# Context projections in feature blocks of 128 and 64, two batches' rests side by side in the array, and a reordered way into layer f1

## The chip, the cores and the metric

The kernel runs on one core of a Trainium2 chip. The metric is the device time of one launch in microseconds (us), the median of several runs. The engines are TensorE (PE), VectorE (DVE), ScalarE (ACT), GpSimd (POOL) and SyncE (SP, which issues most transfers); the profile also has PEld, the weight loads of TensorE.

## The reference

Two blocks of a gated cross-attention network over 8 batches of 100 tokens with 256 features, and a context of 361 rows with 192 features per batch. What the change touches, cut to its core:

```python
# block 0: cross-attention on the layer-normed tokens
q = x @ Wq + bq                                  # 16 heads of 16
k = y @ Wk + bk ; v = y @ Wv + bv                # y: (8, 361, 192), Wk and Wv: (192, 256)
attn = softmax(q k / 4) ; out = relu((attn v) @ W1 + b1) @ W2 + b2
# then a top-1 mixture of 8 experts (256 -> 1024 -> 256)
# block 1: bitnet_linear(x, W, b): int8 activations (one scale for the whole tensor), ternary weights
vis = bitnet_linear(y, W_d2v)                    # 192 -> 256
image = bitnet_linear(vis, W_img) ; fused = bitnet_linear(x, W_txt)
for Wa in (W_att0, W_att1): kv = bitnet_linear(image, Wa) ; fused += 0.1 * softmax(fused k) k
h = relu(bitnet_linear(concat(fused, mean(image)), W_f1)) ; bitnet_linear(h, W_f2)
# then attention whose q, k, v, o are mixtures of 16 experts
```

## The kernel before

Every engine has its own instruction stream, written out by hand; semaphores join them. There is no scheduler: the order in the code is the order on each engine.

**The front** (the first 61 us). SP issues the loads in the order keys' weights `w_k`, context of batch 0, values' weights `w_v`, batch 1, tokens `x`, batches 2 and 3, constants, `w_q`, batches 4 to 5 and 6 to 7, then the ternary layers' weights. The context lies transposed in `ctx_a`, its 192 features in two blocks (k = 0, 1) of `KC` = 96 partitions. TensorE makes the keys of a batch in two halves m (`project_keys`, a 128x361 output each) and the values in three chunks `CH` of some 120 context rows (`project_values`, 121x256 each). Each of these five outputs of a batch takes two fp32 matmuls, one for each feature block; the profile shows each fp32 matmul as two instructions. The outputs go round banks 0 to 3, and ACT copies each out (`context_keys_out`, `context_values_out`). Batches 0 to 3 come first, with the transposes of the normalised tokens (`turn_tokens`) in between, then the queries, then batches 4 to 7 with the score waves of batch 0 between them. `score_wave(b, w)` makes four score blocks of 100x361 at the same time, each on 32 of the array's 128 rows and in a bank of its own; DVE takes maxima from them (`score_maxima`), and the next wave waits for these. `split_maxima` makes three bf16 parts of the maxima, `turn_maxima` transposes them. After batch 0's split, DVE also makes the ternary form of `f2`.

Meanwhile DVE makes the layer norm of the tokens, the largest absolute context value (`ctx_maximum`), the ternary weights, and the quantised context `qc` (`quantise`: a pass into fp32, a pass into bf16). POOL spreads the queries of a batch over head blocks (`spread_q`).

**The loop** (61 to some 190 us): for n = 0 to 9, `score_pair` (two 64-row matmuls of 400 columns side by side, fp32, then two in bf16 from `rows_bf`), the four waves of the next batch, `values`, and between them up to six `chain_unit`s: the d2v layer (16 units, each two bf16 matmuls from `qc`, K = 96) in n = 0 to 2 and the img layer in n = 5 to 7.

**Into f1** (381 us). DVE adds the last attention outputs to `fT` (`add_out`), takes their maximum (`token_maximum`), POOL reduces it over the partitions, DVE rounds tokens and the mean of the image (`qavg`) and f1's 16 outputs follow on TensorE, each four bf16 matmuls: two from `qx`, two from `qavg`. `keep_busy(0, 8)` has TensorE do 8 matmuls that nobody reads while it waits.

## Time and profile before

| | us |
|---|---|
| three runs | 598.03, 600.60, 601.18 (median 600.6) |
| the profiled execution's own time | 597.44 |
| its span, first to last instruction | 595.3 |
| TensorE busy in the span | 579.1 (97%) |
| VectorE, ScalarE, GpSimd busy | 385.1 (65%), 219.2 (37%), 138.2 (23%) |

A timeline line gives the start and the length of a merged run of equal instructions, the engine, the source line, the output and inputs by name, the shape, and how many; in square brackets stands how long the engine was idle before it and which instruction ended that. Lengths of matmuls overlap, since they are pipelined, so the time that a piece takes is read from one start to the next.

### The profile page before, as it was taken

Reading aid. Unit: us, or ns where it says so; the run is one execution under the profiler, and the core shown is the slowest. Engines: PE = TensorE matmul, PEld = TensorE weight load, DVE = VectorE, ACT = ScalarE, POOL = GpSimd, SP = SyncE. Lnnn points to the kernel's source line nnn. Section 1 sums busy time; section 2 is a strip of 40 time slices with the busy share of each in tenths; the row PEclk is TensorE's granted clock in tenths of the full one; section 3 lists DMA queues with packets and bytes.
Section 4 is the critical chain, followed back from the end, with each engine's and each line's share of the span. In section 5 each row is a group of like instructions: output and inputs, shape, how many; then the busy total and the mean of one; then the engine's idle time right before and its main releaser. Section 6 shows DMA issues by size and latency. Waiting matters only on the chain.

```text
span 595.3 us, 10362 instructions
## 1 busy us (share of the span) xinstructions
PE 579.1 (97%) x3975; PEld 429.9 (72%) x3975; DVE 385.1 (65%) x928; ACT 219.2 (37%) x513; POOL 138.2 (23%) x172
## 2 busy tenths in 40 slices
PE   9989999999999999999999989999999999999997
PEld 7756344454456767999999748767787888887587
DVE  2895767587884865222222579887999779775454
ACT  3554656566673464222222376585210010001000
POOL 0052201114003402222222000004355565440000
PEclk9999999999999999999999999999999999999999
DMA  8920000012000662999998200610743663320000
GB/s 193 325 87 1 18 2 1 4 35 57 2 1 22 207 216 69 312 339 354 350 340 276 64 1 1 207 42 2 243 139 96 209 220 95 106 80 0 1 28 29
DMA packets 25694, 71.07 MB, mean 119 GB/s; under 512 B 5270, under 2 KB 13062, under 8 KB 21814
## 3 DMA queue, kind: packets, MB, share of 16 engines
q1 hardware_dynamic: 21910, 58.15, 29.7%
q0 software_dynamic: 3744, 12.38, 6.3%
q8 instruction: 27, 0.44, 0.3%
q14 instruction: 13, 0.11, 0.1%
HBM read 65.02 MB, written 5.49 MB: 118 GB/s over the span
## 4 chain that ended last, share of the span: by engine, by line
PE 83%; DVE 12%; ACT 3%; issue 2%; POOL 1%; DVEq 0%; POOLq 0%
PE bank L1666 12%; PE bank L2190 10%; PE bank L1998 8%; PE bank L2011 8%; PE bank L1821 8%; PE bank L2268 7%; PE bank L2178 6%; PE bank L1795 5%; PE bank L1839 3%; PE bank L1764 2%; PE bank L1827 2%; PE bank L1645 1%; DVE nmax L1063 1%; PE bank L2118 1%; PE bank L2115 1%
## 5 line engine op out<-in xcount | busy, mean ns | idle before, releaser
L2190 PEld LDWEIGHTS bank<-region,kvT 128*128 128x128 f32 x448 | 77.0, 190 | 9.9 <-issue 0.9
L2190 PE MATMUL bank<-region,kvT 128*128 128x200 f32 x448 | 81.1, 333 | 0.8 <-DVE region L1180 0.8
L761 DVE TENSOR_REDUCE nmax<-bank 100x2 f32<-100x722 f32 x64 | 55.2, 905 | 24.9 <-PE bank L1795 24.6
L1998 PEld LDWEIGHTS bank<-stage,region 128*128 128x128 f32 x448 | 52.1, 192 | 1.4 <-issue 0.8
L1998 PE MATMUL bank<-stage,region 128*128 128x128 f32 x448 | 52.4, 275 | 0.5 <-ACT stage L1490 0.5
L2011 PE MATMUL bank<-region,stage 128*128 128x256 f32 x224 | 50.7, 379 | 0.0
L2178 PE MATMUL bank<-region,kvT 128*128 128x400 f32 x128 | 48.5, 502 | 0.6 <-DVE region L1187 0.6
L2011 PEld LDWEIGHTS bank<-region,stage 128*128 128x128 f32 x224 | 41.5, 190 | 5.0
L2268 PE MATMUL bank<-region,kvt 128*128 128x200 f32 (+1 forms) x192 | 44.5, 389 | 0.3 <-DVE region L1247 0.3
L977 DVE TENSOR_SCALAR stage<-bank,stage 128x128 f32<-128x128 f32 x56 | 15.8, 344 | 43.6 <-PE bank L1998 43.6
L554 POOL TENSOR_TENSOR kvT<-kvT 128x256 f32<-128x256 f32 x32 | 27.6, 863 | 54.9 <-DMA kvT<-in_p_qkv 47.7
L1513 ACT ACTIVATE stage<-bank,stage 128x128 f32<-128x128 f32 x56 | 16.0, 368 | 66.1 <-PE bank L1998 66.1
L2268 PEld LDWEIGHTS bank<-region,kvt 128*128 128x128 f32 x192 | 33.5, 190 | 9.0 <-DVE region L1247 0.6
L1821 PE MATMUL bank<-xT,kvt 64*121 64x400 f32 (+1 forms) x144 | 37.9, 545 | 0.7 <-ACT region L1469 0.4
L470 POOL PARTITION_ALL_REDUCE scol<-scol x5 | 1.8, 361 | 142.2 <-DVE scol L753 46.8
L1247 DVE TENSOR_TENSOR region<-region,stage 128x200 f32<-128x200 f32 (+1 forms) x48 | 20.3, 435 | 18.8 <-PE bank L2268 18.8
L2178 PEld LDWEIGHTS bank<-region,kvT 128*128 128x128 f32 x128 | 23.1, 190 | 10.9 <-issue 1.1
L1187 DVE TENSOR_TENSOR region<-xT,stage 128x800 f32<-128x800 f32 x30 | 30.8, 1026 | 0.1
L1469 ACT ACTIVATE region<-bank 121x400 f32<-121x400 f32 (+1 forms) x48 | 21.8, 501 | 19.8 <-PE bank L1827 19.8
L983 DVE TENSOR_TENSOR stage<-bank,stage 128x256 f32<-128x256 f32 x14 | 5.9, 425 | 35.6 <-PE bank L2011 35.6
L1469 ACT ACTIVATE kvT<-bank 121x400 f32<-121x400 f32 (+1 forms) x48 | 21.8, 501 | 19.2 <-PE bank L1827 19.2
L526 POOL DMA_INDIRECT y_slots<-stage,token_of x13 | 13.0, 996 | 67.4 <-DVE stage L983 67.4
(360 smaller groups left out, 1097.0 us busy)
## 6 DMA issues: line engine op xcount, KB each, us to landing
region<-in_e_w SPq DMA_DIRECT2D x28, 1024.0 KB, 6.2
kvT<-in_p_qkv SPq DMA_DIRECT2D x32, 384.0 KB, 3.1
stage<-w_dram POOLq DMA_DIRECT2D x2, 1600.0 KB, 13.3
stage<-in_t_f SPq DMA_DIRECT2D x1, 2048.0 KB, 14.6
kvt<-in_p_o SPq DMA_DIRECT2D x1, 2048.0 KB, 9.0
stage<-in_e_b SPq DMA_DIRECT2D x14, 128.0 KB, 6.6
region<-in_ctxT SPq DMA_DIRECT2D x3, 541.5 KB, 13.5
stage<-w_dram POOLq DMA_DIRECT2D x3, 400.0 KB, 4.8
```

The lines of the kernel that those rows point to most:

```text
L554: pool.tensor_tensor(s[:, 0:2, :], w[:, :, HE:2 * HE], w[:, 0, 0:2 * HE].rearrange("p (i n) -> p i n", i=2), ALU.subtract).then_inc(S["poo ...
L761: dve.tensor_reduce(nmax[:, b % 2, at_h:at_h + 9:8], banks[0:N, bank:bank + 2, 0:M], AX.X, ALU.max, negate=True)\
L1187: dve.tensor_tensor(x_w[n % NW], xT[:, :, at_h], w_bc[h][:, None, e, :].to_broadcast([P, 2, HT]), ALU.mult).then_inc(S["xw_done"], 1)
L1469: act.activation(probsT[n % 2][0:rows_c, c, g].rearrange("p j n -> p (j n)"), psum[4 + y % 3][0:rows_c, 0:4 * N], ACT.Exp).then_inc(S["y_o ...
L1666: ins = pe.matmul(bank, w(k), src(k), start=start and k == 0, stop=stop and k == kk - 1)
L1795: ins = pe.matmul(psum[i + (4 if b == 0 else 0)][0:N, 0:M], qm[b % 3][at_i, t, 2 * (i % 2) + par, :], kT[at_i, t, b, :], start=True, stop= ...
L1821: pe.matmul(bank[g], kT[at_g, t, b, c0:c0 + rows_c], qm[b % 3][at_g, t].rearrange("p j n -> p (j n)"), start=True, stop=False)
L1998: ins = pe.matmul(psum[2 * u + m // 4][:, (m % 4) * P:(m % 4 + 1) * P], e_w1[u][:, k, m * P:(m + 1) * P], xsT[u][:, k, :], start=k == 0, s ...
L2011: ins = pe.matmul(psum[4 + u][:, 0:D], hsT[u][:, m, :], e_w2[u][:, m, :], start=m == 0, stop=m == KF - 1)
L2178: ins = pe.matmul(psum[V_BANK[h]][:, 0:HT], p_w[n % NP][:, k, 2 * HE:3 * HE], x_w[n % NW][:, k, :], start=e == 0 and k == 0, stop=e == E1 ...
L2190: return pe.matmul(bank, left, right, start=e == 0 and i % 2 == 0, stop=e == E1 - 1 and i in (1, 3, 5, 6))
L2268: ins = pe.matmul(psum[LAST_BANK[part] + m][:, at_p], o_all[:, e, m * P:(m + 1) * P], z_w[n % NW][:, at_p], start=e == 0, stop=e == E1 - 1)
```

## The change

The 192 features stand in a block of 128 (`ctx_f`, all 8 batches) and a rest of 64 (`ctx_r`). Rests of even batches lie on partitions 0 to 63, those of odd batches on 64 to 127, and the rest of each weight (`w_k`, `w_v`, d2v) is loaded twice, once for each half. `pair_of_banks` works on a pair of batches: two 128-row matmuls into two banks, then the two rests on the two row halves. The order of loads is now: both batches of pair 0, `w_v`, `x`, pair 1, constants, `w_q`, pairs 2 and 3; ACT issues seven of the first loads. The context's maxima and its quantisation go over 128 partitions and 12 blocks of 361 columns instead of 96 partitions and 16 blocks. The d2v units use a 128-row and a 64-row matmul. TensorE no longer waits for `q_out` before pair 2, and `turn_maxima(0)` stands ahead of the first wave of batch 1. The last part changes the way into f1. The diff, cut:

```diff
+KR = DT - P
-for _name, _p, _w in (("d2v", KC, 512), ("img", P, 512), ("txt", P, 512), ("att0", P, 256),
+for _name, _p, _w in (("d2v", P, 512), ("img", P, 512), ("txt", P, 512), ("att0", P, 256),
-CTX_PARTS = ((0, 1), (1, 2), (2, 4), (4, 6), (6, 8))
+PAIRS = B // 2
+CTX_PART = (0, 1, 2, 2)
+        ctx_f = region[:, 0:B * M].rearrange("p (b m) -> p b m", b=B)
+        ctx_r = region[:, B * M:ctx_w].rearrange("p (r m) -> p r m", r=PAIRS)
 # SP
+            def load_context(part, b0, b1):
+                sp.dma_start(ctx_f[0:KC, b0:b1], d["ctxT"][:, 0, b0:b1]).then_inc(S[f"ctx_in{part}"], 16)
+                sp.dma_start(ctx_f[KC:P, b0:b1], d["ctxT"][0:P - KC, 1, b0:b1]).then_inc(S[f"ctx_in{part}"], 16)
+                for s in range(2):
+                    sp.dma_start(ctx_r[s * KR:s * KR + KR, b0 // 2:b1 // 2], d["ctxT"][P - KC:KC, 1, b0 + s:b1:2])\
+                        .then_inc(S[f"ctx_in{part}"], 16)
+            sp.dma_start(w_a[0:KC, 512:768], d["w_a"][0:KC, 512:768]).then_inc(S["ctx_in0"], 16)
+            sp.dma_start(ctx_f[0:KC, 0:2], d["ctxT"][:, 0, 0:2]).then_inc(S["ctx_in0"], 16)
+            for s in range(2):
+                sp.dma_start(ctx_r[s * KR:s * KR + KR, 0], d["ctxT"][P - KC:KC, 1, s]).then_inc(S["rest_in0"], 16)
...
 # DVE
-            layernorm(ins)
-            for part in range(1, len(CTX_PARTS)):
-                ins = ctx_maximum(part)
-            link(ins)
+            layernorm(ins, lambda: ctx_maximum(1))
+            link(ctx_maximum(2))
-            quantise(qc[0:KC], ctx_a[0:KC], kvT[0:KC, :, :, :], 0, KC).then_inc(S["quantised"], 1)
+            quantise(stage[:, 4096:6984].bitcast(BF16)[:, 0:ctx_w], region[:, 0:ctx_w], kvT_cols[:, 0:ctx_w], 0)\
+                .then_inc(S["quantised"], 1)
-                if 4 <= n < 2 * B + 4:
-                    add_out(dve, n - 4)
                 if n >= 5:
                     g = n - 5
                     if g < B:
                         token_sum(g)
                     else:
                         ins = token_maximum(g - B)
+                if 4 <= n < 2 * B + 4:
+                    add_out(dve, n - 4)
...
-            dve.tensor_scalar(half_of(q_tmp, 0), half_of(fT, 0), scol[:, 19:20], MAGIC, ALU.mult, ALU.add)
+            link(dve.tensor_scalar(half_of(q_tmp, 0), half_of(fT, 0), scol[:, 19:20], MAGIC, ALU.mult, ALU.add))
+            dve.tensor_scalar(half_of(qx, 0), half_of(q_tmp, 0), MAGIC, None, ALU.subtract)\
+                .then_inc(S["half_rounded"], 1)
             dve.tensor_scalar(avg[:, :, :], avg[:, :, :], scol[:, 19:20], MAGIC, ALU.mult, ALU.add)
             output_scale(16, ("f1",))
-            dve.tensor_scalar(qavg, avg[:, :, :], MAGIC, None, ALU.subtract)
-            dve.tensor_scalar(half_of(qx, 0), half_of(q_tmp, 0), MAGIC, None, ALU.subtract)\
-                .then_inc(S["half_rounded"], 1)
+            dve.tensor_scalar(qavg, avg[:, :, :], MAGIC, None, ALU.subtract).then_inc(S["half_rounded"], 1)
 # PE
+            def pair_of_banks(r, unit, rows_c, width, left, right):
+                for s in range(2):
+                    j = 10 * r + 2 * unit + s
                     if j >= 4:
                         pe.wait_ge(S["ctx_out"], j - 3)
+                    pe.matmul(psum[j % 4][0:rows_c, 0:width], left(slice(0, P), 0, 2 * r + s),
+                              right(slice(0, P), 0, 2 * r + s), start=True, stop=False)
+                if r == 0 and unit == 0:
+                    pe.wait_ge(S["rest_in0"], 64)
+                for s in range(2):
+                    j, at_s = 10 * r + 2 * unit + s, slice(s * KR, s * KR + KR)
+                    pe.matmul(psum[j % 4][0:rows_c, 0:width], left(at_s, 1, r), right(at_s, 1, r),
+                              start=False, stop=True).then_inc(S["ctx_mm"], 1)
 # PE, chain_unit
+                    elif k == 0:
+                        at_k, moved = slice(0, P), q_f[:, b, :]
+                    else:
+                        at_k = slice(b % 2 * KR, b % 2 * KR + KR)
+                        moved = q_r[at_k, b // 2, :]
 # PE, the second half of the front
-            pe.wait_ge(S["q_out"], 4)
-            project_context(4)
+            project_keys(2)
+            project_values(2)
             score_wave(0, 0)
-            project_context(5)
+            project_keys(3, (0,))
...
             score_wave(0, 1)
-            project_keys(6)
+            project_keys(3, (1,))
             score_wave(0, 2)
-            project_values(6)
+            project_values(3, (0, 1))
             score_wave(0, 3)
-            project_context(7)
+            project_values(3, (2,))
+            pe.wait_ge(S["consts_bf"], 2)
+            turn_maxima(0)
 # PE, into f1
-            keep_busy(0, 8)
+            keep_busy(0, 6)
...
-                    pe.wait_ge(S["half_rounded"], 3 + half)
+                    pe.wait_ge(S["half_rounded"], 3 + 2 * half)
...
+                if n == 0:
+                    pe.wait_ge(S["half_rounded"], 4)
```

ACT copies out two banks per unit instead of one, in the same order as TensorE makes them; DVE sums the absolute d2v weights in two reductions, one of which leaves out the second copy of the rest.

## Rows read from the trace of the kernel before

**Rows 1.** The page, busy time of each engine.

```profile
PE 579.1 (97%) x3975; PEld 429.9 (72%) x3975; DVE 385.1 (65%) x928; ACT 219.2 (37%) x513; POOL 138.2 (23%) x172
```

**Rows 2.** Timeline of TensorE, 5 to 61 us.

```profile
5.67 2.59 PE L1666 MATMUL bank<-region,w_a 96*128 96x361 f32 x8
8.10 2.75 PE L1666 MATMUL bank<-w_a,region 96*121 96x256 f32 x12
10.69 2.59 PE L1666 MATMUL bank<-region,w_a 96*128 96x361 f32 x8
...
15.70 2.59 PE L1666 MATMUL bank<-region,w_a 96*128 96x361 f32 x8
...
23.15 1.54 PE L1638 MATMUL bank<-consts,xn 100*128 100x100 f32 x16
...
27.13 5.54 PE L1666 MATMUL bank<-xT,w_a 128*128 128x400 f32 x16
33.35 2.69 PE L1666 MATMUL bank<-region,w_a 96*128 96x361 f32 x8 [0.68 <-ACT xn L1382]
...
39.81 0.87 PE L1795 MATMUL bank<-kvt,xT 32*100 32x361 f32 x8 [1.17 <-POOL xT L488]
40.61 2.69 PE L1666 MATMUL bank<-region,w_a 96*128 96x361 f32 x8
43.14 2.75 PE L1666 MATMUL bank<-w_a,region 96*121 96x256 f32 x12
...
53.24 0.87 PE L1795 MATMUL bank<-kvt,xT 32*100 32x361 f32 x8
...
59.79 0.87 PE L1795 MATMUL bank<-kvt,xT 32*100 32x361 f32 x8 [0.46 <-ACT stage L1360]
...
60.87 0.94 PE L1821 MATMUL bank<-xT,kvt 64*121 64x400 f32 x4
```

**Rows 3.** Timeline of TensorE in the loop, 64 to 67 us.

```profile
64.40 0.87 PE L1795 MATMUL bank<-kvt,xT 32*100 32x361 f32 x8
65.20 0.94 PE L1821 MATMUL bank<-xT,kvt 64*121 64x400 f32 x4
65.97 0.34 PE L1827 MATMUL bank<-kvT,rows_bf 64*121 64x400 bf16 x2
66.24 0.48 PE L1764 MATMUL bank<-stage,tern 96*128 96x361 bf16 x2
66.65 1.29 PE L1795 MATMUL bank<-kvt,xT 32*100 32x361 f32 x8
```

**Rows 4.** Windows, 5 to 15 us: busy by engine, clock, DMA share, GB/s.

```profile
5.00:15.00 10.00, 10.00 (x41) 7.46 (x40) 2.59 (x7) 3.94 (x9) 0.00 (x0) 1.00 0.96 221
```

**Rows 5.** Timeline of VectorE, 20 to 61 us.

```profile
20.66 5.58 DVE L689 TENSOR_REDUCE umax<-region 96x1 f32<-96x722 f32 x4
...
35.15 3.22 DVE L672 TENSOR_SCALAR kvT<-region,scol 96x5776 f32<-96x5776 f32 x1
38.41 4.37 DVE L673 TENSOR_SCALAR stage<-kvT 96x5776 bf16<-96x5776 f32 x1
...
54.15 1.73 DVE L761 TENSOR_REDUCE nmax<-bank 100x2 f32<-100x722 f32 x2 [1.85 <-PE bank L1795]
...
56.60 0.23 DVE L774 TENSOR_TENSOR small<-nres,small 100x16 bf16<-100x16 f32 x1
...
60.73 1.72 DVE L761 TENSOR_REDUCE nmax<-bank 100x2 f32<-100x722 f32 x2
```

**Rows 6.** Timelines of TensorE and VectorE ahead of f1.

```profile
381.55 3.72 PE L1645 MATMUL bank<-consts 128*128 128x256 f32 x16 [0.52 <-DVE stage L364]
385.11 0.50 PE L2115 MATMUL bank<-stage,tern 128*128 128x400 bf16 x2
...
381.41 0.62 DVE L1056 TENSOR_REDUCE umax<-stage 128x1 f32<-128x200 f32 x2
...
384.23 0.57 DVE L1092 TENSOR_SCALAR stage<-region 128x800 bf16<-128x800 f32 x1
```

More of the change, by code:

```diff
@@ L89 @@
 TERN_NAMES = list(TERN)
[L92 to L94 removed]
+TERN_SIZE = {_name: _p * _w for _name, (_p, _w, _) in TERN.items()}
+TERN_SIZE["d2v"] = DT * D
+PAIRS = B // 2
+CTX_PART = (0, 1, 2, 2)
 RAW = {"f1": 0}
```

156 lines of the change are left out of this document (83 added, 73 removed).

## The prediction, made before the changed kernel was run

> **What bounds the kernel now.** I read the page's busy times first, then TensorE's timeline, then the waits of the front. TensorE is busy for 579.1 of 595.3 us [rows 1], so only time that TensorE saves, or idle time that goes, can move the end. In the front TensorE works without a stop from 5.67 us to the queries, and then idles three times: 0.68 us for the queries' copies, 1.17 us for GpSimd's spread queries, 0.46 us for a bank [rows 2], 2.3 us in all. The loop's first `score_pair` starts at 60.87 us [rows 2]; how much earlier it starts is the first term of my sum.
>
> **The context units, the bulk of the change.** Keys of a batch are four fp32 matmuls in 8.10 - 5.67 = 2.43 us, 0.61 each; values are six in 10.69 - 8.10 = 2.59 us, 0.43 each [rows 2]. Eight batches cost 8 x 5.02 = 40.2 us. A new unit serves two batches: two full matmuls and two rests side by side, so three matmul times instead of four: 1.82 us for a keys unit (2.43 before), 1.30 us for a values unit (1.73 before). With 8 and 12 such units that alone would be 30.1 us, a saving of 10.1.
>
> That two 64-row matmuls do run side by side is seen: `score_pair`'s two of 400 columns take 65.97 - 65.20 = 0.77 us [rows 3], and one after the other they would take 2 x 0.61 x 400/361 = 1.35. But they take 0.10 more than one (0.67), and this excess is everywhere that the number of rows in use changes. Four 32-row matmuls of a wave take 0.80 instead of 0.61; the bf16 pair takes 0.27 instead of 0.67/4 = 0.17; the d2v unit behind it 0.41 instead of 2 x 0.61/4 = 0.30 [rows 3]; keys just after a wave take 43.14 - 40.61 = 2.53 instead of 2.43 [rows 2]. I read it as 0.1 us for leaving one row split and 0.1 us for starting fp32 work in the next, whose first weights can't be loaded beforehand. A new unit goes from 128 rows to 64 and back: 0.4 us. So a keys unit costs 2.22, a values unit 1.70, four pairs of batches 4 x (2 x 2.22 + 3 x 1.70) = 38.2 us: a saving of 2.0 us instead of 10.1. The bounds are no cost for the change of split (10.1 saved) and 0.19 above mine, the whole excess of a wave with its four tiles (0.59 per unit, 1.8 lost).
>
> The Trainium skill (TensorEngine Tiling (Array Packing), Theoretical Speedup) has up to 2x for contractions of at most 64 rows, which by itself would give the 10.1 us. The same page (Key Properties) says that changing the tiling mode drains TensorE, without a price; the trace agrees, with about 0.1 us for each change. That rule speaks against a scheme that changes the split 40 times.
>
> **The front's timeline after.** A wave between two context units changes the split anyway, so the 0.2 us that a unit already pays for its way back are not paid again: 0.7 us saved over four waves. The copies of the weights' rests add 2 x 64 KB ahead of `x`; at 221 GB/s [rows 4] that is 0.6 us. The first unit now needs 0.5 MB instead of 0.46; I start TensorE at 6.0 us. Pair 0 ends at 6.0 + 9.5 = 15.5. Batches 2 and 3 had landed by 15.70 [rows 2], exactly when no idle time is seen, so they may have been there sooner; 0.6 us later is 16.3 at the latest, and I take 16.0. From there: keys 4.4, two values units 3.4, token transposes 1.4, a values unit 1.7, queries 5.5 [rows 2], pair 2 9.5: wave (0,0) starts at 41.9, later than before (39.81), but with six batches done, not five.
>
> VectorE must have quantised by then. Its maxima go over 12/16 of the columns (5.58 us plus the first batch's become some 4.9, half of it before the token normalisation), the quantisation's 3.22 + 4.37 = 7.59 becomes 5.7 [rows 5]. The weights' work between them, 8.9 us from 26.24 to 35.15, grows by one small reduction, and they land later by the 0.19 MB of copies, 0.8 us. So quantising still starts at about 35.2 and ends at 40.9 instead of 42.78, ahead of TensorE by 1 us. Spread queries are no longer late either: the queries come at 32.7, as before, but 9 us of context work lie ahead of the wave.
>
> Then wave 0.8, keys 2.2, the sum and wave (0,1) 1.3, keys 2.2, wave 0.8, two values units 3.4: wave (0,3) starts at 52.8. TensorE would be through the last values unit at 55.3. But `turn_maxima(0)` has been moved ahead and now waits for the split, which ended 56.83 - 53.24 = 3.6 us after the start of wave (0,3) [rows 2, 5]: 56.4. The wave behind it is queued on that wait. This wait of 1.1 us is new; before, batch 7's whole projection covered it. Transpose and wave take 60.87 - 59.79 = 1.1 [rows 2]: `score_pair` starts at 57.5 instead of 60.87, **3.4 us earlier**.
>
> **What is late next.** Behind the split VectorE makes f2 ternary until its next maxima at 60.73, 3.9 us after the split's end [rows 5]: now 56.4 + 3.9 = 60.3. The second half of wave (1,1) may start when these two maxima of 1.72 together are out, 62.05. Wave (1,1) comes 64.40 - 60.87 = 3.5 us after the pair [rows 2, 3], at 61.0. **1.0 us is given back** here; before there were 2 us to spare.
>
> **The d2v units.** Their second matmul moves from 96 to 64 rows, a change of split inside each of the 16 units. Where a `score_pair` follows (about 5 of them) it is only moved; in the other 11 it adds 0.1, in bf16 with nothing to reload: **1.0 us lost**, between 0 and 1.7 (if fp32 loads behind it are exposed too).
>
> **Into f1.** One maximum of 0.3 us leaves the chain (the last two took 0.62), and the rounded half no longer stands behind the mean and scale, some 0.5 us in all; `keep_busy` ends 2 x 0.43 us sooner. Before, both ended at about 385.0, and f1 started at 385.11 [rows 6]. Now the half is there at about 384.3, f1's first two matmuls follow, and the next two wait for `qavg` until about 384.9, where before they began two bf16 matmuls of 0.17 behind f1's start, at 385.45: **0.6 us saved** (bounds 0.3 and 0.8). The 32 matmuls, ACT's copies and VectorE's maxima are each paced by TensorE there, so the shift is kept.
>
> **Costs at nothing.** ACT's seven issues stand ahead of its first copy, needed only by the third unit at 10.4 us, 4 us after the first; if they took that long, TensorE would wait. ACT's copies now come two at a time; ACT is busy for 3.94 of 10 us there [rows 4] with two batches' copies, so a values unit's two fit into its 1.7 us. Everything from 190 us on keeps its order, except the loop ahead of f1, where a sum and an add change places in a stream that has the same length.
>
> **Sum.** 3.4 - 1.0 - 1.0 + 0.6 = 2.0 us faster. The profiled execution of 597.44 would become 595.4; against the median of 600.6 it is 598.6. The profiled execution is 3.2 us under that median, so a measured difference has some noise of its own: 0.5% (3.0 us) is about what can be told from no change.
>
> **Rivals.**
> - *The changes of split are nearly free* for this accumulating form. At 0.2 us per unit instead of 0.4, wave (0,0) would come at 39.7 and VectorE's quantising (40.9) would lead; the pair would start near 54.4, and with 1.0 lost behind it, 0.5 on d2v and 0.6 won: 5.6 faster, 595.0. For it: the rests of a unit lie in banks that are already open. Against: every row of rows 3 shows 0.1. At no cost at all the waits on VectorE hold the gain at 6.6: 594.0. Chance 0.2.
> - *New waits eat it*: pair 1 lands at 18 instead of 16, or copies hold back banks: 1.5 to 2.5 less, 600.4. For it: the pair's data is now four transfers, the last of which counts, and TensorE reaches it in the one spell in which the DMA share is 0.96 [rows 4]. Chance 0.2.
> - *Slower*: TensorE's wait for pair 1 grows until the granted clock falls from 2.4 to 1.2 GHz. It is full in all windows after the start [rows 4], and the idle times stayed at 1.2 us or less [rows 2]. A wait of 4 us (landing at 19.5) costs 3.5 beyond the forecast, and then 3 to 4 us of work at half clock cost as much again: 604. [...] Or the split costs 0.6 per unit: 4 us more, 602.6. Together 0.1.
> - The forecast, 596.8 to 600.2: chance 0.5.
>
> **How the numbers follow.** Faster by over 0.5% (below 597.6): the first rival and about a third of the forecast's own range, 0.37. Slower by over 0.5% (above 603.6): the last rival, with a little noise, 0.11. Within: 0.52. The range from 594.0 (no cost of the split) to 602.0 leaves out most of the last rival and a little at the other end. The forecast's own range is 596.8 to 600.2.
>
> **What would show it.** Keys units of 2.2 us and values units of 1.7 us between starts, with the rests' two matmuls starting together; TensorE idle behind pair 0 until about 16; `turn_maxima(0)` idle behind VectorE's split and `score_pair` at 57.5; wave (1,1) idle behind VectorE's maximum; f1's first matmul at 0.7 us after the time that the shift of the loop gives. The prediction is wrong if values units take 1.4 or 2 us, or if the time before pair 1 is over 2 us.

## The result, and the profile after

The changed kernel took 606.59 us (median of 6 runs, 604.33 to 607.35), the kernel before 599.36 us beside it (6 runs, 597.46 to 601.18): a ratio of 1.0116 [1.0093, 1.0139], 1.2% slower. I had forecast 598.6 us with 602.0 as the upper end. The forecast had the wrong sign, and the time lies outside the range. The profiled execution took 604.33 us with a span of 602.0; before it was 597.44 and 595.3, so 6.7 us of span are to be found. One launch of a later run, r9_group, at 819.9 us with a mean granted clock of 0.752, is in a slower state of the chip and is left out of its ratio.

The page of the kernel after, busy times and TensorE's clock in 40 slices:

```profile
PE 583.3 (97%) x3971; PEld 421.7 (70%) x3971; DVE 383.6 (64%) x930; ACT 217.5 (36%) x513; POOL 134.5 (22%) x172
PEclk9999699999999999999999999999999999999999
```

TensorE is busy for 4.2 us more than in [rows 1], although the units have fewer full passes. One digit of the clock row shows why: in the fifth slice (60 to 75 us) the granted clock was about two thirds. The windows of the kernel after (length; busy time by engine; granted clock, DMA share, GB/s) have a second such place:

```profile
12.00:16.00 4.00, 3.49 (x9) 2.00 (x10) 2.71 (x8) 1.99 (x5) 0.00 (x0) 0.57 1.05 238
...
60.00:75.00 15.00, 13.41 (x58) 4.62 (x58) 8.40 (x12) 5.42 (x13) 0.00 (x0) 0.66 0.02 6
```

In these stretches the clock was at 1.2 GHz instead of 2.4 for part of the time. The trace's clock records give 12.57 to 15.98, 60.35 to 63.77 and 67.18 to 74.01 us, together 13.7 us at half clock, which cost up to 6.8 us of work. The other launches had no less: the mean granted clock is 0.989 in the three that took 604.33, 604.71 and 606.22 us, and 0.983 in the three that took 606.96 to 607.35, which is some 7 us more at half clock. So the profile shows the milder case.

TensorE's timeline of the kernel after, which answers [rows 2] and [rows 3]; a square bracket is a wait and its releaser:

```profile
5.98 1.38 PE L1707 MATMUL bank<-region,w_a 128*128 128x361 f32 x4
...
12.51 1.99 PE L1707 MATMUL bank<-w_a,region 128*121 128x256 f32 x4 [2.13 <-ACT kvt L1382]
...
19.12 1.48 PE L1707 MATMUL bank<-region,w_a 128*128 128x361 f32 x4
...
21.34 1.48 PE L1707 MATMUL bank<-region,w_a 128*128 128x361 f32 x4
...
23.56 1.12 PE L1707 MATMUL bank<-w_a,region 128*121 128x256 f32 x4
...
25.24 1.12 PE L1707 MATMUL bank<-w_a,region 128*121 128x256 f32 x4
...
44.81 0.87 PE L1837 MATMUL bank<-kvt,xT 32*100 32x361 f32 x8
...
60.53 0.49 PE L1850 MATMUL bank<-ident_bf,small 100*128 100x100 bf16 x4 [2.36 <-DVE small L793]
60.95 1.54 PE L1837 MATMUL bank<-kvt,xT 32*100 32x361 f32 x8
62.42 1.58 PE L1863 MATMUL bank<-xT,kvt 64*121 64x400 f32 x4
64.99 0.38 PE L1869 MATMUL bank<-kvT,rows_bf 64*121 64x400 bf16 x2 [0.98 <-ACT kvT L1483]
...
81.18 0.35 PE L1850 MATMUL bank<-ident_bf,small 100*128 100x100 bf16 x4
```

The units at full clock cost what I had summed up: a keys unit 21.34 - 19.12 = 2.22 us, a values unit 25.24 - 23.56 = 1.68. The time is in three waits, 2.13, 2.36 and 0.98 us, and in what stands at half clock around them: the wave at 60.95 took 1.47 us to `score_pair`'s start where [rows 3] has 0.80.

Who held TensorE stands in the timeline of ScalarE, kernel after:

```profile
3.77 1.14 ACTq L1343 DMA_DIRECT2D w_a<-in_w_a  x2
...
11.71 0.20 ACT L1403 ACTIVATE cols<-cols 128x2 f32<-128x2 f32 x1 [5.41 <-DMA w_a<-in_w_a]
11.82 1.90 ACT L1382 ACTIVATE kvt<-bank,cols 128x361 f32<-128x361 f32 x4
...
64.44 0.49 ACT L1483 COPY kvT<-bank 128x400 bf16<-128x400 bf16 x1 [3.99 <-DVE tern L745]
```

and of VectorE and GpSimd around the split, the kernel after:

```profile
58.52 1.35 DVE L791 TENSOR_TENSOR nres<-nmax,small 100x16 f32<-100x16 f32 x1
...
62.01 2.35 DVE L745 SCALAR_TENSOR_TENSOR tern<-region,wabs,tern 128x2048 bf16<-128x2048 f32 x1
```

```profile
58.29 1.55 POOL L503 TENSOR_TENSOR w_a<-xn,consts 128x800 f32<-128x800 f32 x1 [10.15 <-PE bank L1713]
```

In the kernel before, the end of f2's ternary form (VectorE), the same GpSimd instruction, and `turn_maxima(1)` (TensorE):

```profile
58.46 2.35 DVE L726 SCALAR_TENSOR_TENSOR tern<-region,wabs,tern 128x2048 bf16<-128x2048 f32 x1
```

```profile
59.41 2.78 POOL L488 TENSOR_TENSOR w_a<-xn,consts 128x800 f32<-128x800 f32 x1 [10.79 <-PE bank L1666]
```

```profile
74.44 0.35 PE L1808 MATMUL bank<-ident_bf,small 100*128 100x100 bf16 x4
```

*The first wait.* ACT's stream begins with a wait for `w_kv_in` at 80, a semaphore that now counts `cols` and all four pieces of `w_v`. ACT issued the last two pieces itself at 3.77 us, beside SP's `x` (3.96), and the last of the four landed at 11.7. Until then ACT copied nothing, four banks were full at 10.3, and the third unit waited for a bank.

*The second wait.* The split's first subtraction took 1.35 us; before it took 0.18. GpSimd's `spread_q` of batch 2 starts with the end of the last context unit; that end now falls into the split, where before GpSimd started at 59.41 us, 2.6 us behind the split's end at 56.83 [rows 5].

*The third wait.* ACT copies the transposed maxima only after a wait for `tern_ready` at 5, that is for f2's ternary form, since the probabilities that this copy leads to overwrite the raw f2. f2 was finished at 64.36 us, ACT had idled 3.99 us, and the two bf16 matmuls of the pair wait for the copy. In the kernel before f2 was ready at 58.46 + 2.35 = 60.8 us, when the pair began, and ACT's copy ran at 61.05.

The account of the whole: `score_pair` started at 62.42 us instead of the 57.5 forecast, 4.9 us late: the first wait and its half clock (2.1 + 1.7, less the 0.5 that I had set down as a wait for pair 1, and some slack) delayed wave (0,0) by 2.9 us (44.81 instead of 41.9), the subtraction added 1.2, the slow wave 0.7. Behind it `turn_maxima(1)` came 81.18 - 62.42 = 18.76 us after the pair, where before it came 74.44 - 60.87 = 13.57 after: 5.2 us, of which 1.0 is the third wait and some 4.1 the 8.2 us at half clock. At `turn_maxima(1)` the kernel is 6.7 us late against before. From there on it loses the 0.75 us that the d2v units still cost (forecast), loses another 0.3 us until f1's fillers that I can't name, and wins 0.64 on the way into f1 (forecast): f1 starts 392.29 - 385.11 = 7.2 us late. Another 0.5 us comes back behind f1, which I can't name either. Steps of 0.2 to 0.6 us at such places also stand between the traces of r6, r9 and r10, whose code is the same there.

TensorE ahead of f1 in the kernel after, for [rows 6]:

```profile
389.37 2.86 PE L1677 MATMUL bank<-consts 128*128 128x256 f32 x12 [0.52 <-DVE stage L371]
392.29 0.50 PE L2158 MATMUL bank<-stage,tern 128*128 128x400 bf16 x2
```

### The profile page after: what moved, and what is told of

Same layout as the page of the kernel before. It is cut to its first block, busy times and chain, and to the rows that moved or that the text cites. A ratio compares the mean times of both kernels' runs of the same rounds, so it can differ in the third digit from the quotient of the medians.

```text
span 602.0 us, 10370 instructions
## 1 busy us (share of the span) xinstructions
PE 583.3 (97%) x3971; PEld 421.7 (70%) x3971; DVE 383.6 (64%) x930; ACT 217.5 (36%) x513; POOL 134.5 (22%) x172
## 4 chain that ended last, share of the span: by engine, by line
PE 79%; DVE 10%; ACT 6%; DMA 3%; issue 1%; ACTq 1%; DVEq 0%; SPq 0%; POOL 0%
PE bank L2235 12%; PE bank L2054 8%; PE bank L1863 7%; PE bank L2041 7%; PE bank L2313 7%; PE bank L2223 7%; PE bank L1698 6%; PE bank L1837 5%; PE bank L1707 3%; PE bank L1881 3%; PE bank L1806 2%; PE bank L1713 2%; PE bank L1869 2%; ACT region L1587 2%; DMA stage<-in_e_b 1%; DMA w_a<-in_w_a 1%
## 5 line engine op out<-in xcount | busy, mean ns | idle before, releaser
L2235 PEld LDWEIGHTS bank<-region,kvT 128*128 128x128 f32 x448 | 77.0, 190 | 10.3 <-issue 0.9
L1545 ACT ACTIVATE stage<-bank,stage 128x128 f32<-128x128 f32 x56 | 16.0, 368 | 67.9 <-PE bank L2041 41.9
L1863 PE MATMUL bank<-xT,kvt 64*121 64x400 f32 (+1 forms) x144 | 39.3, 565 | 0.4 <-ACT kvT L1501 0.2
L2223 PEld LDWEIGHTS bank<-region,kvT 128*128 128x128 f32 x128 | 23.1, 190 | 10.4 <-issue 0.6
```

The lines of the kernel that those rows point to most:

```text
L1863: pe.matmul(bank[g], kT[at_g, t, b, c0:c0 + rows_c], qm[b % 3][at_g, t].rearrange("p j n -> p (j n)"), start=True, stop=False)
L2223: ins = pe.matmul(psum[V_BANK[h]][:, 0:HT], p_w[n % NP][:, k, 2 * HE:3 * HE], x_w[n % NW][:, k, :], start=e == 0 and k == 0, stop=e == E1 ...
L2235: return pe.matmul(bank, left, right, start=e == 0 and i % 2 == 0, stop=e == E1 - 1 and i in (1, 3, 5, 6))
```

## The experiments

All ratios are to the kernel before in runs beside it, with a 95% interval. Spans and clocks are those of the one profiled execution.

### One cause at a time

**r1_cols.** Change: ACT no longer waits for the weights.

```diff
-            sp.dma_start(cols[:, 0:24], d["cols"]).then_inc(S["w_kv_in"], 16)
+            sp.dma_start(cols[:, 0:24], d["cols"]).then_inc(S["cols_in"], 16)
...
-            act.wait_ge(S["w_kv_in"], 80)
+            act.wait_ge(S["cols_in"], 16)
...
-            pe.wait_ge(S["w_kv_in"], 80)
+            pe.wait_ge(S["w_kv_in"], 64)
```

> The changed kernel, but ACT waits for the bias columns alone (a semaphore of their own) and no longer for the last piece of the values' weights, which landed at 11.7 us. Theory A (the loss is two waits of TensorE, 2.13 us ahead of the third unit and 2.36 us ahead of turn_maxima(0), and the half clock that follows each): ACT copies from about 7 us on, TensorE waits only for the weights themselves, from 10.3 to 11.7, 1.3 us instead of 2.1; if that is short enough for the clock to stay full, 0.8 + up to 1.7 us come back (ratio to the kernel before 1.008 to 1.010), if not 0.8. Theory B (the split units by themselves look idle to the clock, waits or not): the stretch at half clock at 12.6 us stays where it is. Theory C (the loss lies in fixed prices of units): time unchanged within 0.5 us.

Measured: 605.43 us, ratio 1.0103 [1.0061, 1.0144], not told apart from the changed kernel. ACT copied from 7.70 us on, but TensorE met the same landing itself, and it came 1 us later in this execution, so the wait that I had expected at 1.3 us was 2.85 (TensorE's timeline):

```profile
12.74 1.13 PE L1707 MATMUL bank<-w_a,region 128*121 128x256 f32 x4 [2.85 <-DMA w_a<-in_w_a]
```

So the late landing is the cause, and ACT's wait only its messenger. The clock stayed full after this wait: 1.00 in the window from 12 to 16 us. It fell at 59.34 us, behind the wait for the split, for 3.4 us. The profiled execution (600.29 us, clock 0.997) is the fastest of its five; the others took 603.3 to 606.4 us at 0.986 to 0.992, so most of the 4 us that it is faster than the changed kernel's profiled execution is not the edit's.

**r2_wv.** In addition all four pieces of `w_v` are issued by SP ahead of `x`:

```diff
+            sp.dma_start(w_a[KC:P, 1024:1280], d["w_a"][0:P - KC, 1280:1536]).then_inc(S["w_kv_in"], 16)
+            for s in range(2):
+                sp.dma_start(w_a[s * KR:s * KR + KR, 1280:1536], d["w_a"][P - KC:KC, 1280:1536])\
+                    .then_inc(S["w_kv_in"], 16)
             sp.dma_start(x[:, :, :], d["x"].rearrange("b n d -> n b d")).then_inc(S["x_in"], 16)
...
-            act.dma_start(w_a[KC:P, 1024:1280], d["w_a"][0:P - KC, 1280:1536]).then_inc(S["w_kv_in"], 16)
-            for s in range(2):
-                act.dma_start(w_a[s * KR:s * KR + KR, 1280:1536], d["w_a"][P - KC:KC, 1280:1536])\
-                    .then_inc(S["w_kv_in"], 16)
```

> As r1_cols, and all four pieces of the values' weights issued by SP ahead of x instead of three of them by ACT beside x. Theory A: they land by 9 us, TensorE runs from 6 us to the queries without a stop, the clock stays full up to turn_maxima(0), pair 0 ends at about 15.6 instead of 19.1 and pair 1's data (landed by 16.5) costs up to 1 us: 2.5 to 3.5 us faster than the changed kernel at the queries. As the wait ahead of turn_maxima(0) stays, the whole is 1.005 to 1.008 of the kernel before. Theory B: half clock at about 12.6 us all the same, gain 2 us at most. Theory C: unchanged but for the 2.1 us of the wait.

Measured: 602.72 us, 1.0054 [1.0032, 1.0076]. The first wait is gone, pair 0 ended at 15.3 us, and now pair 1 is late: it landed at 17.50, inside the 16 to 18 that one of my rivals had priced (TensorE's timeline):

```profile
17.50 1.48 PE L1707 MATMUL bank<-region,w_a 128*128 128x361 f32 x4 [2.23 <-DMA region<-in_ctxT]
```

The ratio is the expected one, the clock is not: it fell at 19.06 us behind this wait, for 3.4 us, and again from 60.02 to 70.26 us.

**r3_spread.** The changed kernel, with GpSimd's spread queries held until the split is over:

```diff
                 if b == 2:
                     pool.wait_ge(S["ctx_mm"], 5 * B)
+                    pool.wait_ge(S["nm_done"], 1)
```

> The changed kernel, but POOL spreads batch 2's queries only when batch 0's maxima are split (a further wait on nm_done). In the changed kernel that spread began at 58.29 us, and DVE's subtraction inside the split took 1.35 us instead of 0.18. Theory A: the subtraction takes 0.18 again, TensorE waits 1.2 us instead of 2.4 ahead of turn_maxima(0); if the clock then stays full after it, some 5 us of half-clock cost (10.2 us at half clock) go too: 5 to 6 us faster, ratio 1.000 to 1.004. If 1.2 us are still enough for it to fall: 1.2 us faster, 1.009. Theory B: clock as in the changed kernel, 1.2 us. Theory C: 0 to 1.2 us.

Measured: 605.23 us, 1.0099 [1.0067, 1.0132]. The timeline of VectorE and the waits of TensorE (total, times, longest):

```profile
57.28 0.18 DVE L792 TENSOR_TENSOR nres<-nmax,small 100x16 f32<-100x16 f32 x1
...
58.27 2.44 DVE L752 TENSOR_SCALAR tern<-region,ws 128x2048 bf16<-128x2048 f32 x1
```

```profile
PE bank L1870 <- ACT kvT L1484: 3.6, 1, 3.6
PE bank L1708 <- ACT kvt L1383: 3.0, 1, 3.0
...
PE bank L1851 <- DVE small L794: 1.2, 1, 1.2
```

The subtraction is back at 0.18 us and the wait for the split at 1.2, within 0.1 of the forecast's 1.1. But GpSimd's work now falls on f2's first pass, which takes 2.44 us instead of 1.29, and the pair waits 3.6 us for ACT's copy. The clock stayed full to 62.38 us, was half to 69.20, and the 5 to 6 us of my theory A did not come. The time comes from f2's end, so a gain ahead of it is given back. That f2 was the gate became plain here.

**r4_filler.** The changed kernel with unread matmuls in the two first waits:

```diff
             project_keys(0)
+            for _ in range(5):
+                pe.matmul(psum[7][:, 0:D], zero_tile[:, 0:1].to_broadcast([P, P]),
+                          zero_tile[:, None, :].to_broadcast([P, 4, D // 4]), start=True, stop=True)
...
+            pe.wait_ge(S["ctx_out"], 38)
+            keep_busy(0, 5)
             turn_maxima(0)
```

> The changed kernel with five matmuls that nobody reads (2.1 us at full clock) at each of the two waits, behind keys of pair 0 and ahead of turn_maxima(0). They shorten no wait. Theory A: the clock stays full to the end, and 13.65 us at half clock become full: up to 6.8 us less, and 1 us for the copy of the maxima that ran on the same wait stays; ratio 1.000 to 1.003. Theory B: the clock falls as before, or within the split units, and the fillers cost 0 to 1 us: 1.012 to 1.014. Theory C: 1.010 to 1.014, since half clock then hid little.

Measured: 603.90 us, 1.0062 [1.0036, 1.0089], some 3 us less than the changed kernel. I had expected 1.000 to 1.003 if the clock stayed full and 1.012 to 1.014 if it did not; it came between. The data come no earlier (the third unit started at 13.23 us); the gain is clock. Half clock was left only from 65.53 to 72.35 us (clock records), behind the pair's wait, which had no filler and had grown from 0.98 to 2.5 us (timelines of ScalarE and TensorE):

```profile
63.57 0.49 ACT L1483 COPY kvT<-bank 128x400 bf16<-128x400 bf16 x1 [3.98 <-DVE tern L745]
```

```profile
64.11 0.38 PE L1872 MATMUL bank<-kvT,rows_bf 64*121 64x400 bf16 x2 [2.53 <-ACT kvT L1483]
```

**r5_f2early.** The changed kernel with f2's ternary form in two halves, between the maxima of batch 0:

```diff
+            dve.wait_ge(S["sum_read"], 1)
+            thresholds(6, 7)
+            link(ternarise_f2(0))
             score_maxima(0, 2)
+            ternarise_f2(1).then_inc(S["tern_ready"], 1)
             score_maxima(0, 3)
             split_maxima(0)
-            dve.wait_ge(S["sum_read"], 1)
-            thresholds(6, 7)
-            ternarise("f2")
```

> The changed kernel, but DVE makes f2 ternary in two halves between batch 0's score maxima instead of after their split. ACT's stream has a wait on the f2 weights ahead of its copy of the transposed maxima, and the copy came at 64.5 us behind them in the changed kernel. Theory A, sharpened (the end of the front is gated by DVE's f2 work through ACT, so what TensorE saves ahead of it is lost): f2 is done before the split; the copy follows turn_maxima(0) within 0.5 us, the wait of the bf16 pair (0.98 us, 2.5 to 3.6 in the kernels with the other waits mended) is gone, and wave (1,1) does not wait. DVE has 2.3 + 1.9 us of f2 work for gaps of 1.6 and 2.4 us, so the split ends 0.5 to 1 us later than before this edit: turn_maxima(0) at 61 to 61.5. Then the time from turn_maxima(0) to turn_maxima(1) falls from 20.7 us to 14.5 to 17, by whether the clock still falls on the wait ahead: 3 to 5 us faster, ratio 1.003 to 1.007. Rival (the half clock alone counts, the gate costs 1 us): 0.5 to 1.5 us faster, ratio 1.009 to 1.011.

Measured: 602.80 us, 1.0066 [1.0035, 1.0098]. The pair's bf16 matmuls no longer wait (TensorE's timeline):

```profile
61.15 0.49 PE L1858 MATMUL bank<-ident_bf,small 100*128 100x100 bf16 x4 [2.56 <-DVE small L793]
63.05 1.68 PE L1871 MATMUL bank<-xT,kvt 64*121 64x400 f32 x4
64.53 0.36 PE L1877 MATMUL bank<-kvT,rows_bf 64*121 64x400 bf16 x2
...
77.67 0.35 PE L1858 MATMUL bank<-ident_bf,small 100*128 100x100 bf16 x4
```

From `turn_maxima(0)` to `turn_maxima(1)` it took 77.67 - 61.15 = 16.5 us, where the changed kernel took 81.18 - 60.53 = 20.65. The first two waits and the half clock behind each (13.38 to 16.79 and 61.17 to 64.58 us) are still there; the third stretch is gone.

**r12_loads.** The changed kernel with the edits of r1 and r2 and pair 1 of the context ahead of `x`, nothing else:

```diff
+            load_context(1, 2, 4)
             sp.dma_start(x[:, :, :], d["x"].rearrange("b n d -> n b d")).then_inc(S["x_in"], 16)
-            load_context(1, 2, 4)
```

> The changed kernel with the front's loads mended and nothing else: ACT waits for the bias columns alone, values' weights and then pair 1's context ahead of x. With r5_f2early (the gate alone) and r6_all (both) it shares out the loss. Theory A: TensorE runs from 6 us to the last context unit with a wait of 1 us, no half clock before 57 us; wave (0,0) at 42, turn_maxima(0) at 57 to 58 behind DVE's split, then the gate: the copy of the maxima waits for f2 until 61.5, the clock falls behind it. Ratio 1.003 to 1.006, 3 to 5 us faster than the changed kernel and as much slower than r6_all. Rival (the clock fell behind the gate only because it had fallen before): no half clock, ratio 0.999 to 1.001.

Measured: 601.80 us, 1.0027 [1.0004, 1.0049], a little better than the 1.003 to 1.006 expected. The early waits are gone (the clock is 1.00 from 12 to 20 us); what stands behind them is whole, with half clock from 62.87 to 69.69 us (waits of TensorE, then ScalarE's timeline):

```profile
PE bank L1869 <- ACT kvT L1483: 2.5, 1, 2.5
PE bank L1850 <- DVE small L797: 2.4, 1, 2.4
PE bank L1707 <- ACT kvt L1382: 1.2, 1, 1.2
```

```profile
61.50 0.49 ACT L1483 COPY kvT<-bank 128x400 bf16<-128x400 bf16 x1 [3.99 <-DVE tern L749]
```

With r5 it makes a table of two causes: the changed kernel 1.0116, loads mended 1.0027, f2's gate mended 1.0066, both mended (r6, below) 0.9969. From the changed kernel the two single mendings multiply to 1.0116 x (1.0027 / 1.0116) x (1.0066 / 1.0116) = 0.9977, within r6's interval. That fits two separate losses, of some 5.3 and 3.0 us. It does not prove that they are separate: each ratio is known to some 0.3% (2 us), and r6 has r3's edit too.

**r8_undo_turn.** The changed kernel with `turn_maxima(0)` back where it was, behind the first wave of batch 1 (`if n < B` in the loop again). It asks whether moving that call did the harm.

> The changed kernel with the transpose of batch 0's maxima put back behind the first wave of batch 1. The prediction held its move for a wait of its own (1.1 us). Theory A (the gate behind DVE's f2 work decides, not this order): the wave (1,0) of 0.8 us now runs inside the wait for the split, so TensorE's wait ahead of turn_maxima(0) falls from 2.4 to 1.5 us, but the bf16 pair still waits for f2 and ACT until 65: 0 to 0.8 us faster, unless the shorter wait keeps the clock full, then up to 5. Rival (the move caused the wait and so the fall of the clock): 4 us faster or more, ratio 1.005 or less.

Measured: 605.10 us, 1.0094 [1.0064, 1.0123], not told apart from the changed kernel, and above the 1.005 of the rival. The wait for the split fell to 0.68 us, and the pair's wait for ACT grew to 3.33 (TensorE's timeline):

```profile
67.20 0.59 PE L1869 MATMUL bank<-kvT,rows_bf 64*121 64x400 bf16 x2 [3.33 <-ACT kvT L1483]
```

The placing of the call only says which instruction waits for VectorE's chain of split and f2. The profiled execution is the slowest of the four (608.58 us): its first wait was 3.8 us, and one stretch of 3.4 us at half clock lies at 428.6 us, far from the front.

**r7_tail.** The kernel before with the change of the way into f1 alone (`keep_busy(0, 6)`, the sum ahead of `add_out`, the rounded half ahead of the mean).

> The kernel before with the way into f1 alone changed (sum and maximum ahead of the add, rounded half signalled by itself, keep_busy 6, wait for the mean's part inside the first output). Prediction's step: f1's first matmul 3.0 us after keep_busy's start instead of 3.56, 0.6 us faster in all, ratio 0.999. Rival (the gain is lost in f1 or at keep_busy behind it): ratio 1.000, second layer at the same time as before.

Measured: 597.43 us, 0.9985 [0.9969, 1.0002]; in the time of one launch it can't be told from nothing. In the trace it can (TensorE's timeline):

```profile
382.18 2.86 PE L1645 MATMUL bank<-consts 128*128 128x256 f32 x12 [0.52 <-DVE stage L364]
385.10 0.50 PE L2115 MATMUL bank<-stage,tern 128*128 128x400 bf16 x2
```

2.92 us from the fillers' start to f1, 3.56 in [rows 6]: 0.64 us saved.

### All causes mended

**r6_all.** The edits of r1, r2, r3, r5 and r12 together, on the changed kernel.

> All mends together on the changed kernel: ACT waits for the bias columns alone; the values' weights and then pair 1's context ahead of x; batch 2's spread after the split; f2 ternary in two halves between the maxima. Theory A: TensorE runs from 6 us without a wait above 1 us, the clock stays full; pair 0 ends at 15.6, wave (0,0) at 42 as predicted, split at 56.5 to 57.5, score_pair at 58 to 59, no wait behind it, d2v units 1.4 us dearer over n = 0 to 2, f1's start 0.6 nearer: 1.5 to 2.5 us faster than the kernel before, ratio 0.996 to 0.9975. Rival C (the fixed prices are larger than the saving even without waits): ratio 1.000 to 1.003 at full clock.

Measured: 596.55 us, 0.9969 [0.9950, 0.9988]; span 593.0, clock 0.999. TensorE's timeline and the window that answers to the 0.66 above:

```profile
20.63 1.15 PE L1716 MATMUL bank<-w_a,region 128*121 128x256 f32 x4 [1.05 <-ACT kvt L1391]
...
41.90 0.87 PE L1846 MATMUL bank<-kvt,xT 32*100 32x361 f32 x8
...
52.71 0.87 PE L1846 MATMUL bank<-kvt,xT 32*100 32x361 f32 x8
...
56.78 0.34 PE L1859 MATMUL bank<-ident_bf,small 100*128 100x100 bf16 x4 [1.52 <-DVE small L798]
...
57.84 0.94 PE L1872 MATMUL bank<-xT,kvt 64*121 64x400 f32 x4
```

```profile
60.00:75.00 15.00, 14.86 (x90) 6.06 (x88) 10.25 (x18) 9.58 (x20) 1.52 (x1) 1.00 0.00 1
```

This is the timeline that I had forecast for the change itself: wave (0,0) at 41.90 (41.9), wave (0,3) at 52.71 (52.8), `score_pair` at 57.84 (57.5), and the median 1.8 us below before (2.0). The two waits left are VectorE's split, 0.4 us longer than forecast, and a bank that ACT frees late because it stands at the layer norm's square root. Half of the 12 launches are like the profiled one (clock 0.999 or 1.000, 594.8 to 596.2 us); in the other half it is 0.994 to 0.997 and they took 596.9 to 599.0, so in them the clock still fell.

**r9_group.** r6 with both keys units of pairs 0 to 2 together, so that four full matmuls come first and then the four rests: one change of split and back instead of two.

```diff
-                for m in ms:
-                    pair_of_banks(r, m, P, M, lambda p, k, z: w_k[p, k, m * P:(m + 1) * P],
-                                  lambda p, k, z: (ctx_f, ctx_r)[k][p, z, :])
+                for m in ms:
+                    for s in range(2):
+                        ...
+                        pe.matmul(psum[j % 4][:, 0:M], w_k[:, 0, m * P:(m + 1) * P], ctx_f[:, 2 * r + s, :],
+                                  start=True, stop=False)
+                for m in ms:
+                    for s in range(2):
+                        ...
+                        pe.matmul(psum[j % 4][:, 0:M], w_k[at_s, 1, m * P:(m + 1) * P], ctx_r[at_s, r, :],
+                                  start=False, stop=True).then_inc(S["ctx_mm"], 1)
```

> r6_all, but where both keys units of a pair of batches stand together (pairs 0, 1, 2), their four 128-row matmuls come first and their four rests behind them: two changes of the array's split instead of four. If a unit's 0.4 us is the price of its two changes, the two units take 4.0 us instead of 4.4 in each of three pairs; ACT then gets four banks within 1.2 us and the first values unit may wait 0.2 to 0.5 us for it. 0 to 1 us faster than r6_all (ratio to the kernel before 0.995 to 0.997). Rival (the 0.1 us excesses belong to the 64-row matmuls themselves, not to the change): 4.4 us as before, and the waits on top.

Measured: 597.10 us, 0.9973 [0.9952, 0.9994], no different from r6 as a whole. The price of the split is seen in the trace: pair 2's two keys units took 36.84 - 32.79 = 4.05 us, in r6 36.86 - 32.52 = 4.34 (TensorE's timeline of r9, then of r6). One round trip of the split less saves 0.29 us; I had put one at 0.4. It does not reach the end: the wait for a bank is 1.7 us instead of 1.05 and that for the split 2.1 instead of 1.5.

```profile
32.79 2.59 PE L1733 MATMUL bank<-region,w_a 128*128 128x361 f32 x8
...
36.84 1.15 PE L1716 MATMUL bank<-w_a,region 128*121 128x256 f32 x4
```

```profile
32.52 1.38 PE L1716 MATMUL bank<-region,w_a 128*128 128x361 f32 x4
...
36.86 1.12 PE L1716 MATMUL bank<-w_a,region 128*121 128x256 f32 x4
```

**r10_best.** r6, with ACT copying the first keys unit of pair 1 ahead of the square root, and f2's absolute sum and threshold taken ahead of the first maxima:

```diff
+            context_keys_out(1, (0,))
             layernorm_scale()
-            context_keys_out(1)
+            context_keys_out(1, (1,))
...
+            pe.wait_ge(S["f2_abs"], 1)
+            pe.matmul(psum[7][:, 400:402], const("ones"), scol[:, 52:54], start=True, stop=True).then_inc(S["sum_mm"], 1)
             score_wave(0, 0)
```

> r6_all with its two last waits shortened: ACT copies the first keys unit of pair 1 ahead of the square root (TensorE waited 1.05 us for the second), and makes f2's absolute sum right behind the queries, so that DVE has the threshold before the first maxima (TensorE waited 1.5 us for the split). Theory A: both waits under 0.5 us, 1.5 to 2 us faster than r6_all at score_pair, ratio to the kernel before 0.993 to 0.995. Rival: DVE has 12 us of maxima, f2 and split work from the end of its quantising at 42.6 in any order, so the split can't end before 55, 1.5 us gained at most and 0.5 if the copies of pair 2 are held back by f2's sum.

Measured: 595.86 us, 0.9956 [0.9940, 0.9972]; its six runs lie between 595.60 and 596.03. The bank's wait is gone, a wait of 0.5 us for the sum came up in wave (0,0), and the pair starts at 58.43, 0.6 us later than in r6. So the 1.5 to 2 us that I expected over r6 did not come; it is not told apart from r6 (0.9969), but it beats both kernels: its interval lies below 1. At full clock it is no faster than r6: the five of its launches with a clock of 0.999 or 1.000 took 595.6 to 596.0 us, the six of r6 594.8 to 596.2. Its lower median goes with launches that seldom lose clock (one of six, at 0.997, against six of twelve).

**r11_before_f2.** How much of that belongs to the blocks of 128 and 64? The kernel before with f2 early, the held spread queries and the way into f1, but with its own blocks of 96.

> The kernel before with the changed way into f1, f2 made ternary between the maxima and batch 2's spread behind the split: the mends without the blocks of 128 and 64. Before, DVE ended f2 at 60.7 us, just ahead of score_pair at 60.87, so the gate didn't bind. Theory A: nothing but f1's 0.6 us is gained, ratio 0.998 to 0.999, about 1.5 us behind r6_all: the blocks are worth that much once nothing waits. Rival (the blocks are worth nothing, r6_all won by its mends): ratio 0.996 to 0.997, as r6_all.

Measured: 597.66 us, 0.9979 [0.9963, 0.9996], beside r10's 595.86 in the same comparison; all of r10's runs are below the lowest of r11's (596.29). So the blocks, with their loads in order and r10's two last edits, are worth some 1.8 us in the median, and the edits that r11 has too about 1.3 (0.21% of 598.8). The profiled execution of r11 shows that the kernel before lives close to the same edge (TensorE's timeline, and the window from 16 us):

```profile
19.11 5.18 PE L1675 MATMUL bank<-region,w_a 96*128 96x361 f32 x8 [3.31 <-DMA region<-in_ctxT]
```

```profile
16.00:20.00 4.00, 0.89 (x2) 0.63 (x3) 3.34 (x16) 1.49 (x2) 0.00 (x0) 0.83 1.05 220
```

The context of batches 2 and 3 came 3.3 us late in that one execution, TensorE fell to half clock (18.63 to 25.46 us in the clock records), and the run took 602.45 us.

## Why the prediction was wrong, point by point

- **Cost of a unit: right.** 2.22 and 1.68 us against 2.22 and 1.70. The rival that the changes of split are nearly free is out. r9 measured one round trip at 0.29 us, so my 0.1 + 0.1 for each change is of the right size and a little high. The single records of the unit at 19.12 us show both parts: successive matmul instructions start 0.30 us apart, but 0.39 to 0.40 apart across each change of rows and 0.41 apart behind the first one after it; and where the weight loads inside a block start some 0.3 us ahead of their matmul, the first behind a change starts together with it (20.53 us). The rule of the Trainium skill (TensorEngine Tiling (Array Packing), Key Properties) that a change of tiling mode drains TensorE agrees with the trace. The two-batches-at-once scheme gave a fifth of what its instruction count promised.
- **The step that failed first is "Costs at nothing".** I had named the event: ACT's first copy is needed by the third unit at 10.4 us, "if they took that long TensorE would wait". I thought of the issuing, which was over at 4.9 us, and not of the landing behind it: ACT's stream opens with a wait that the change raised from 32 to 80, and the pieces that it then waits for were issued together with `x`. They landed at 11.7 us. r1 and r2 show that it is the landing: with ACT freed of the wait, TensorE waited for the same pieces; with the pieces ahead of `x`, nobody did. I priced at zero what cost 2.1 us and the half clock behind it.
- **Pair 1 at 16.0: right only as long as others were late.** In the changed kernel it was never waited for, since pair 0 ended late; VectorE read it at 16.76 us without a wait, so it was there by then. When pair 0 ended at 15.3 us (r2), pair 1 came at 17.50, nearer to the rival's 18 than to my 16.0. Ahead of `x` (r6, r12) it was no longer waited for.
- **Wave (0,3) at 52.8: a slip in the sum.** The steps from 41.9 add up to 10.7 us, so to 52.6, and the forecast should have read 0.2 us faster. r6 measured 52.71.
- **VectorE's quantising: 1.4 us later than forecast, at no cost.** I had it end at 40.9 us; it ran from 36.17 to 42.30 us in the changed kernel and to 42.6 in r6. In r6 VectorE still idled 0.22 us for wave (0,0) behind it, so only 0.2 us of my 1 us of room was left.
- **Split 3.6 us behind wave (0,3): wrong by 1.2.** I moved the last context unit next to the split and did not look at what GpSimd starts when that unit ends. r3 shows it by removing it: 0.18 instead of 1.35 us for the subtraction, 1.2 instead of 2.4 for TensorE's wait.
- **"What is late next": the second failed step.** I saw that f2's ternary form would end later against TensorE, and charged it 1.0 us, at wave (1,1), through VectorE's maxima. I followed VectorE's own stream and left out who else waits for `tern_ready`: ACT, ahead of its copy of the transposed maxima, on which the pair right behind `turn_maxima` depends. Before, f2 was done at 60.8 us and ACT's copy began at 61.05, so the gate was open just in time and left no row in the waits. What TensorE gained against VectorE's chain it lost again in waiting: 0.98 us in the changed kernel, 2.5 to 3.6 where something ahead was mended (r3, r4, r8, r12), none where f2 was early (r5, r6). With the loads in order and f2 left where it was (r12) the kernel was still 0.27% slower than before; the 1.0 us that I had charged was the wrong wait on the wrong engine.
- **The slower rival had the right mechanism at the wrong place.** I let the granted clock fall only from a 4 us wait for pair 1 on. It fell behind waits of 2.1 and 2.4 us on other engines. The fall added 1.7 us to the first wait's 2.1, and the 6.8 us at half clock that began 2.2 us behind the third wait cost 3.4 us, where the wait itself was 0.98. That the waits brought it about is shown by their removal: with fillers in the first two only the stretch behind the third was left (r4), and with the waits at 1.5 us or less there was none in the profiled execution (r6). The rival's price does not add up either: 3.5 us beyond the forecast and as much again is 605 to 606 us, not 604; that the measured 606.59 is near this sum is luck, since no wait for pair 1 was in it. 0.11 for all ways to be over 603.6 us was too little for a timeline that had put TensorE up against three engines at once.
- **d2v units: right.** From one `turn_maxima` to the next it takes 16.54 us instead of 15.99 and 15.50 instead of 15.30, and r6 against before 14.94 instead of 13.85, of which 0.80 is a wave that now lies inside: 0.55 + 0.20 + 0.29 = 1.0 us, as forecast.
- **Into f1: right.** 0.64 us in the changed kernel and in r7, 0.6 forecast. It is too small for the whole time to show.
- **The whole sum** would have held with the loads and f2 in order: r6's 1.8 us against 2.0. That the numbers agree so well is partly chance, since r6 also has edits that the forecast had not.
- **The signs of being wrong did not fire.** I had named values units of 1.4 or 2 us and more than 2 us ahead of pair 1. The units took 1.68 us and nothing waited for pair 1, and the forecast was wrong all the same: the signs covered the terms of the sum and not the gates that I had put at nothing.

What is left open: where the half clock lies in the launches that have no profile. Their mean clocks are on record (0.989 or 0.983), their places are not. Nor is it shown why one wait lowers the clock and a longer one does not.

## What to carry to other kernels

When a change makes the bounding engine arrive earlier, walk every semaphore that guards the reuse of a buffer as if it were a data dependence, on every engine's stream: a gate that opened just in time leaves no row in the waits, and becomes the next bound at once. When a change raises the count of a wait or moves a small load behind a big one, price the landing and not the issue, and ask which first instruction of which engine stands behind it. In these runs a wait of 2 us on TensorE was not priced at 2 us: r4's unread matmuls in two waits won some 3 us, and half clock behind a wait cost 1.7 us (3.4 us long) or 3.4 us (6.8 us long). And compare a profiled execution with the median and the clocks of the other launches before reading a gain from it: r1's profiled execution was 4 us faster than the changed kernel's, while the two ratios differ by 0.1%.

## What the runs showed of the hardware

- **The clock after a short wait.** TensorE's granted clock fell from 2.4 to 1.2 GHz behind waits of 2.13 us (the changed kernel), 2.23 (r2) and 2.56 (r5), and did not behind one of 2.85 us (r1; the window from 12 to 16 us has 1.00) nor one of 3.0 (r3, the same window, 1.00), nor one of 2.4 (r12, ahead of `turn_maxima(0)`), nor one of 2.1 (r9). The length of the wait alone doesn't decide it in these traces. Within one kernel the times go with the mean granted clock, if not strictly: five of r5's seven launches took 599.22 us at 0.995, 601.41 at 0.994, 602.80 at 0.991, 604.37 at 0.989 and 605.72 at 0.984, but r1 has 605.60 at 0.992 beside 603.32 at 0.988.
- **VectorE beside GpSimd.** A subtraction of 100x16 took 1.35 us instead of 0.18 while GpSimd multiplied 128x800, and a pass over 128x2048 from fp32 to bf16 took 2.44 instead of 1.29. The Trainium skill (GPSIMD Engine Reference, Key points) says that GpSimd shares its SBUF interfaces with VectorE and that the two contend when VectorE's instruction has two SBUF inputs or runs in a 2-port mode; the trace agrees, by row, for the subtraction, which has two SBUF inputs. Both were delayed by some 1.2 us, however different their own lengths; the GpSimd instruction beside the subtraction took 1.55 us and ended at 59.84, the subtraction at 59.87. In r5 a cast of 100x16, with one input, took 1.26 us instead of 0.20 beside it. It works the other way round too: in the kernel before, GpSimd's instruction started 0.95 us into f2's second pass and took 2.78 us instead of 1.52, while that pass kept its 2.35. In all four rows the instruction that started second is the one held up.
- **Small loads beside a big one.** Pieces of `w_v` issued by ACT at 3.77 us landed at 11.7 us in the changed kernel and at about 12.7 in r1, with the DMA share at 0.95 from 5 to 12 us. The Trainium skill (DMA: Bandwidth & Descriptors, Issuing engines are not separate DMA queues) says that transfers started by several engines run on the same DMA engines and interleave, and that a second issuing engine saves only the time to issue; the trace agrees: ACT's issue at 3.77 us brought the pieces no priority over `x`.
